# Storing two images interleaved, column by column, so that a depthwise matmul reads 8 rows of 64 instead of 16 rows of 32

## What is computed

```python
# x: (8, 32, 64, 64) f32
xd    = concat of x[:, :, i::2, j::2] for i, j in (0,1)      # (8, 128, 32, 32), of the group-normalised x
feats = concat([dwconv(xd, w1, 1), dwconv(xd, w3, 3), dwconv(xd, w5, 5)], axis=1)   # depthwise, zero padding
y     = einsum('bchw,oc->bohw', feats, w_proj[:, :, 0, 0])   # 384 -> 128 channels
out   = x + (the four 32-channel parts of y put back on the even/odd rows and columns)
```

## Time and profile before

| | us |
|---|---|
| median of 3 runs | 147.49 (147.2 to 148.9) |
| span of the profiled execution | 147.0 |
| PE / DVE / ACT / POOL busy | 133.2 / 117.4 / 103.0 / 98.2 |

### The profile page before, as it was taken

One profiled execution on the slowest core, in us unless ns is written; L12 is line 12 of the kernel. 1 busy time (PEld: TensorE's weight loads), 2 busy tenths in 40 slices (PEclk: granted clock), 3 DMA queues, 4 the chain that ended last, 5 costly groups with the idle time before them and its releaser, 6 DMA issues.

```text
span 147.0 us, 1502 instructions
## 1 busy us (share of the span) xinstructions
PE 133.2 (91%) x513; PEld 98.8 (67%) x513; DVE 117.4 (80%) x132; ACT 103.0 (70%) x110; POOL 98.2 (67%) x73
## 2 busy tenths in 40 slices
PE   0478699999999999999999999999999999999960
PEld 0324487788776777678768777777777778777820
DVE  0198999996299999999999999799929996993051
ACT  2295999999956998699869986998799750005000
POOL 7104799999699529994999399649984998001910
PEclk9999999999999999999999999999999999999997
DMA  3999993052052016001509599025194990936946
GB/s 97 217 207 211 207 210 52 0 112 46 0 116 38 0 38 116 0 4 38 114 2 212 109 196 200 7 51 101 36 214 75 185 195 17 214 76 135 195 99 143
DMA packets 35432, 15.73 MB, mean 107 GB/s; under 512 B 34017, under 2 KB 34145, under 8 KB 35041
## 3 DMA queue, kind: packets, MB, share of 16 engines
q1 hardware_dynamic: 33408, 8.39, 31.6%
q0 software_dynamic: 1440, 7.04, 24.7%
q10 hardware_dynamic: 576, 0.21, 0.6%
HBM read 4.41 MB, written 4.19 MB: 59 GB/s over the span
## 4 chain that ended last, share of the span: by engine, by line
PE 86%; DVE 4%; DMA 3%; ACT 2%; ACTq 1%; issue 1%; DVEq 1%; POOL 0%; POOLq 0%
PE YP L551 76%; PE YP L594 9%; DMA w_sb<-in_L_conv_w_dram 3%; DVE st L424 2%; DVE X L522 1%; ACT G L340 1%; DVE weff L449 1%; DVEq L86 0%; PE SMALL L539 0%; ACT HI L384 0%; PE SMALL L533 0%; POOL rstd L253 0%; ACTq L311 0%; ACTq L312 0%; ACTq L310 0%
## 5 line engine op out<-in xcount | busy, mean ns | idle before, releaser
L275 POOL TENSOR_TENSOR RING_SUM<-RING_SUM,PROD 128x900 f32<-128x900 f32 (+1 forms) x37 | 75.1, 2030 | 7.8 <-ACT PROD L365 3.9
L489 DVE SCALAR_TENSOR_TENSOR ACC<-G,coef,ACC 128x930 f32<-128x930 f32 (+1 forms) x62 | 74.2, 1197 | 2.0
L551 PE MATMUL YP<-LO,whi 128*128 128x512 f32 (+1 forms) x154 | 41.6, 419 | 0.0
L551 PE MATMUL YP<-HI,whi 128*128 128x512 f32 (+1 forms) x154 | 40.1, 411 | 1.4 <-ACT HI L384 1.4
L551 PE MATMUL YP<-HI,wlo 128*128 128x512 f32 (+1 forms) x154 | 38.9, 401 | 0.0
L551 PEld LDWEIGHTS YP<-HI,whi 128*128 128x128 f32 x154 | 30.2, 197 | 10.2 <-DVE whi L468 2.6
L365 ACT ACTIVATE PROD<-G,coef 128x900 f32<-128x900 f32 (+1 forms) x37 | 36.2, 1056 | 0.0
L551 PEld LDWEIGHTS YP<-LO,whi 128*128 128x128 f32 x154 | 29.2, 190 | 10.1 <-issue 3.4
L551 PEld LDWEIGHTS YP<-HI,wlo 128*128 128x128 f32 x154 | 29.1, 190 | 7.2
L375 ACT ACTIVATE Y<-YP 64x1024 f32<-64x1024 f32 x14 | 15.3, 1094 | 23.9 <-PE YP L594 23.8
L340 ACT ACTIVATE G<-X,nbias,rstd 64x1024 f32<-64x1024 f32 (+2 forms) x18 | 21.9, 1214 | 2.1 <-DVE nbias L442 1.7
(11 more groups left out here) (55 smaller groups left out, 57.3 us busy)
## 6 DMA issues: line engine op xcount, KB each, us to landing
LO<-G POOLq DMA_DIRECT2D x7, 543.0 KB, 4.9
X<-in_x_dram SPq DMA_DIRECT2D x12, 256.0 KB, 5.4
X<-Y POOLq DMA_DIRECT2D x3, 1024.0 KB, 7.0
out_dram<-X SPq DMA_DIRECT2D x12, 256.0 KB, 5.9
X<-in_x_dram SPq DMA_DIRECT2D x8, 128.0 KB, 4.3
out_dram<-X SPq DMA_DIRECT2D x8, 128.0 KB, 2.2
wp_sb<-in_L_conv_w_proj_dram ACTq DMA_DIRECT2D x1, 192.0 KB, 3.4
w_sb<-in_L_conv_w_dram ACTq DMA_DIRECT2D x1, 12.5 KB, 3.9
```

The costliest lines, as they stand in the source:

```text
L275: pool.tensor_tensor(dst, dst, prod(b, k), ALU.add).then_inc(prod_added, 1)
L489: dve.scalar_tensor_tensor(part(ACC, tap), g_tap(b, tap), of5(tap), part(ACC, tap), ALU.mult, ALU.add).then_inc(acc_step, 1)
L551: mm = nc.tensor.matmul(dst, w[:, n, :], src, start=start, stop=False, skip_group_check=True)
```

## The change

- `G`, `HI` and `LO` have two slots of a pair each in place of four slots of an image each. The two images of a pair are interleaved: element (row, column, image), so a row is 64 elements (`ROW`) at a pitch of 68, and a tap's column shift is 2 elements per column.
- The unit of work is half of a pair's rows: unit u = 2t is rows 0 to 15 of both images of pair t, unit 2t + 1 rows 16 to 31. A unit has as many columns as an image had, two banks of 8 rows of 64.
- `normalise(t)` handles a pair with four instructions, writing every second element; `split(t)` handles a pair with one instruction for `HI` and one for `LO`; `low_part(t)` has one DMA for a pair. Pair 0 is normalised in three parts, of 9, 8 and 15 rows.
- `copy_y(u)` has four instructions of half the size (64 x 512), reading every second element of PSUM. DVE's and SP's last steps are in twice as many parts of half the size for the lower rows.
- The order on ACT becomes the one shown below: one `normalise`, `split` for two units, and each `copy_y` has a new place.

```diff
-            for b in range(1, B):
-                if b >= 3:
-                    copy_y(b - 3)
-                if b in (2, 4):
-                    act.wait_ge(stats_ready, b // 2 + 1)
-                normalise(b, 0, PH, g_ready)
-                split(b)
-                products(b)
-            copy_y(B - 3)
-            copy_y(B - 2)
+            normalise(0, 0, TOP, g_top)
+            high_part(0, 0, TOP, g_top, 4, hi_top)
+            normalise(0, TOP, MID, g_mid)
+            high_part(0, TOP, MID, g_mid, 4, hi_mid)
+            normalise(0, MID, PH, g_ready)
+            high_part(0, MID, PH, g_ready, 4, hi_ready)
+            products(0)
+            products(1)
+            act.wait_ge(stats_ready, 2)
+            normalise(1, 0, PH, g_ready)
+            split(1)
+            products(2)
+            copy_y(0)
+            products(3)
+            for t in range(2, PAIRS):
+                copy_y(2 * t - 3)
+                if t == 2:
+                    act.wait_ge(stats_ready, 3)
+                normalise(t, 0, PH, g_ready)
+                split(t)
+                products(2 * t)
+                copy_y(2 * t - 2)
+                products(2 * t + 1)
+            copy_y(UNITS - 3)
+            copy_y(UNITS - 2)
...
+            def copy_y(u):
+
+                act.wait_ge(conv_done, u + 1)
+                t, r0 = u // 2, UH * (u % 2)
+                if t >= 2 and u % 2 == 0:
+                    act.wait_ge(row_added[t - 2], 16)
+                yp = YP[:, u % 2, :].rearrange("p (h w b) -> p h w b", w=PW, b=2)
+                for par in range(2):
+                    for j in range(2):
+                        act.activation(Y[HALF * par:HALF * (par + 1), t % 2, r0:r0 + UH, :, j],
+                                       yp[HALF * j:HALF * (j + 1), :, :, par], ACT.Copy).then_inc(y_copied, 1)
...
# add_tap, first tap of units 0 and 1 on DVE
-                    dve.wait_ge(g_ready, 2 * b + 2)
+                    dve.wait_ge(g_ready, 4 * (b // 2) + 4)
...
# tap_matmuls
-                    r0, r1 = span(dy, bank * BANK_ROWS, (bank + 1) * BANK_ROWS)
-                    src = image(tile, b, (r0 + dy) * PITCH + 2 + dx, r1 - r0)[:, :, c0:c1]
-                    dst = YP[:, b % 2, r0 * PW:r1 * PW].rearrange("p (r c) -> p r c", c=PW)[:, :, c0:c1]
+                    r0, r1 = span(dy, base + bank * BANK_ROWS, base + (bank + 1) * BANK_ROWS)
+                    src = pair(tile, t, (r0 + dy) * PITCH + 2 * (2 + dx), r1 - r0)[:, :, c0:c1]
+                    dst = YP[:, b % 2, (r0 - base) * ROW:(r1 - base) * ROW].rearrange("p (r c) -> p r c", c=ROW)[:, :, c0:c1]
...
# high(b)
-                    for bank, rows_ready in enumerate([hi_top, hi_ready]):
+                    for bank, rows_ready in enumerate([hi_top, hi_mid]):
...
-                    pe.wait_ge(hi_ready, b + 1)
+                    pe.wait_ge(hi_ready, b // 2 + 1)
                     if b >= 2:
-                        pe.wait_ge(y_copied, 2 * (b - 1))
+                        pe.wait_ge(y_copied, 4 * (b - 1))
```

More of the change, by code:

```diff
@@ L45 @@
 N_PROD = [len(taps) - 1 for taps in POOL_OF]
[L46 removed]
+PROD_SIZE = UH * ROW
 LATE = (0, 1)
@@ L82, in span, with unit_rows, unit_cols @@
     return max(lo, -d), min(hi, PH - d)
+def unit_rows(u, dy):
+    r0 = UH * (u % 2)
+    lo, hi = span(dy, r0, r0 + UH)
+    return lo - r0, hi - r0
+def unit_cols(dx):
+    c0, c1 = span(dx, 0, PW)
+    return 2 * c0, 2 * c1
 def build(nc, x, w1, w3, w5, wp, out):
@@ L331, in _ @@
             act.activation(whi[:, N_INNER:N_PE, :], weff[:, N_INNER:N_PE, :], ACT.Copy).then_inc(extra_ready, 1)
-            def normalise(b, r0, r1, done):
-                if b >= SLOTS:
-                    act.wait_ge(f_ready, b - SLOTS + 1)
-                    act.wait_ge(lo_ready[b - SLOTS], 16 if b > SLOTS else 1)
-                t, p0 = b // 2, HALF * (b % 2)
-                rows = X[p0:p0 + HALF, t, r0:r1, :].rearrange("p h (w j) -> p h w j", j=2)
-                for j in range(2):
-                    act.activation(g_image(b, r0, r1)[HALF * j:HALF * (j + 1)], rows[:, :, :, j], ACT.Identity,
-                                   bias=nbias[p0:p0 + HALF, t:t + 1],
-                                   scale=rstd[p0:p0 + HALF, t:t + 1]).then_inc(done, 1)
@@ L368, in copy_y, with normalise @@
-            def copy_y(b):
-                act.wait_ge(conv_done, b + 1)
-                if b >= 4:
-                    act.wait_ge(row_added[b // 2 - 2], 16)
-                p0 = HALF * (b % 2)
-                for j in range(2):
-                    act.activation(Y[p0:p0 + HALF, b // 2 % 2, :, :, j],
-                                   YP[HALF * j:HALF * (j + 1), b % 2, :].rearrange("p (h w) -> p h w", w=PW),
-                                   ACT.Copy).then_inc(y_copied, 1)
+            def normalise(t, r0, r1, done):
+                if t >= SLOTS:
+                    act.wait_ge(f_ready, 2 * (t - SLOTS) + 2)
+                    act.wait_ge(lo_ready[t - SLOTS], 16 if t > SLOTS else 2)
+                for par in range(2):
+                    p0 = HALF * par
+                    rows = X[p0:p0 + HALF, t, r0:r1, :].rearrange("p h (w j) -> p h w j", j=2)
+                    for j in range(2):
+                        dst = g_image(t, r0, r1)[HALF * j:HALF * (j + 1)].rearrange("p r (c b) -> p r c b", b=2)
+                        act.activation(dst[:, :, :, par], rows[:, :, :, j], ACT.Identity,
+                                       bias=nbias[p0:p0 + HALF, t:t + 1],
+                                       scale=rstd[p0:p0 + HALF, t:t + 1]).then_inc(done, 1)
@@ new lines, in products @@
+            def products(u):
+                if u - SUMS in LATE:
+                    act.wait_ge(f_ready, u - SUMS + 1)
+                elif u > SUMS:
+                    act.wait_ge(acc_step, steps_before(u - SUMS) + 1)
+                act.activation(RING_SUM[:, u % SUMS, :, :], g_tap(u, POOL_OF[u][0], True), ACT.Copy,
+                               scale=of5(POOL_OF[u][0])).then_inc(first_prod, 1)
+                for k in range(N_PROD[u]):
+                    if products_before(u) + k >= PRODS:
+                        act.wait_ge(prod_added, products_before(u) + k - PRODS + 1)
+                    act.activation(prod(u, k), g_tap(u, POOL_OF[u][k + 1]), ACT.Copy,
+                                   scale=of5(POOL_OF[u][k + 1])).then_inc(prod_ready, 1)
@@ L611, in _ @@
             pe.wait_ge(whi_ready, 1)
-            for b in range(B):
+            for b in range(UNITS):
                 high(b)
```

211 lines of the change are left out of this document (107 added, 104 removed).

## The result

The changed kernel takes 156.96 us (median of 4 runs, 156.54 to 157.77); the kernel before, run beside it on the same chip, takes 148.19. The ratio is 1.060, 95% interval 1.054 to 1.067; ratios compare the means of a kernel's fast runs, without runs more than 1.5% above its fastest, so they can differ a little from the ratio of the medians. The profiled execution has a span of 155.5 us where that of before has 147.0: 8.5 us more. The forecast was 154.0, in a range of 150.5 to 158.5.

What follows compares the result with a forecast made beforehand. PE's matmul spacing was taken to bound the kernel. `high(2)` at 54.4, `high(4)` 85.0, `high(6)` 115.6, `ring(7)` 145.95 and the tail gave a span of 153.5, 6.5 more; on the median 147.49 that is 154.0 us, range 150.5 to 158.5.

Steps and rivals of the forecast that it cites:

- The direction and its mechanism: Whole kernel: slower, 6.5 us more, with PE idle before `high(2)`, `high(4)` and `high(6)` until released by ACT's copy.
- ACT's chain: ACT's queue from `ring(2t - 3)` to `high(2t)`: copies, normalise, split and six products, 20.45 us, and 0.1 to release PE.
- The two unknown forms: Normalise's strided writes and the copy's strided PSUM reads on ACT: nothing added; upper bound for the reads 0.58 us a unit.
- Length of the pauses: PE's waits at `high(4)` and `high(6)` for ACT's copies: about 2.8 us each.
- PE's own part: PE from that ring to `high(2t)`: low 4.06, high 8.13, ring 1.72, low 4.06, in all 17.97 us.
- The start: Up to `high(2)`: pair 0 normalised whole and pair 1's scale late, so `high(2)` starts at 54.4, 4.85 us late.
- The matmuls: PE's tap matmuls: half the row breaks save 13.4 ns each, a unit's taps taking 12.19 us instead of 12.91.
- the rows cost nothing: Rival on PE's tap matmuls: they don't get faster, + 192 x 13.4 ns, 156.6 us; chance 0.10.
- The tail: From `ring(7)` to the end: DVE's eight smaller adds 3.5 us instead of 2.85, stores smaller, +0.55 us.
- The clock: Rival on PE's new pauses: each brings 3 us at 1.2 GHz, three cost 4.2 us, 158.2 us; chance 0.10.
- pairs: From `high(2)` to `high(4)` and on to `high(6)`: 30.6 us a pair, where two images took 29.24.
- last stretch: From `high(6)` to `ring(7)`, PE setting the pace: 31.94 us less 120 matmuls of 13.3 ns, 30.35 us.

Runs made afterwards that it cites:

- the pattern experiment: The changed kernel with the nine inner taps of units 1 to 7 reading different patterns of 512 elements; one unbroken run took 232 ns a matmul, no kernel time given.
- e10_widths: The changed kernel with the inner taps of units 1 to 7 reading one aligned contiguous run, 256 to 512 elements wide; matmuls of 256 columns stood 118 ns apart.

## Why the prediction was right, point by point

**The direction and its mechanism: right.** PE pauses before `high(2)`, `high(4)` and `high(6)`, each released by `copy_y`; taking each place away gives the time back.

**ACT's chain: right.** Worked out 20.45 us and 0.1 for PE, measured 20.26 and 0.14. Strided writes and strided PSUM reads cost nothing to speak of: copies of 512 start every 0.65 us (four in 2.59), where 0.67 was taken. The two unknown forms at the lower bound were the right choice.

**Length of the pauses: a third too long.** 2.8 us foreseen, 1.72 and 1.83 measured. The chain on ACT was right; PE's own part was worked out with matmuls that are too fast. With 12.74 instead of 12.19 us a unit PE's 16.25 us of tap matmuls become 16.98, and ACT's chain was 0.19 shorter: 2.8 - 0.73 - 0.19 = 1.9. So the pauses came out shorter than foreseen through the error in the matmuls, not through one in the queue. The pair took 30.87 and 30.96 us for 30.6.

**The start: right in kind, 1.5 us too long.** `G` was complete and DVE began at 23.17 (23.6 foreseen); PE waited 1.76 us at the combine (2.7); ACT waited for the scale of pair 1:

```profile
36.13 5.45 ACT L370 ACTIVATE G<-X,nbias,rstd 64x1024 f32<-64x1024 f32 x4 [2.38 <-DVE nbias L484]
```

at 36.13 for 37.5 foreseen. From the first tap to the end of the scale DVE took 12.93 us instead of the 13.78 carried over from before, where one short instruction between the taps (`dev`, 128 x 1) had taken 1.40 us; here it took 0.16, against which stood a wait of 0.44 for POOL's rstd. That one term makes 0.85 of the 1.5 us, the first tap 0.4, and ACT's own chain most of the rest.

**The matmuls: wrong, the step that failed.** "I take 13.4, since the contiguous record has no such excess": that was a record of the ring's f32 matmuls, taken for the rounded type of the taps. An unbroken run of the taps' type costs 232 ns by the pattern experiment, not 216, so 16 of the 27 ns put down to the rows were never theirs, and of the rest only part goes, since the shifted taps left the 16-byte boundary. A unit gained 0.17 us, not 0.72. The rival "the rows cost nothing", 156.6 with a chance of 0.10, hit the measured 156.96 in its sum, though not for its reason: rows do cost, by where they start. The Trainium skill (Advanced Engine Details and Errata, SBUF Cachelines) has lines of 16 bytes in SBUF and a penalty when each access goes to a different one; the boundary seen here agrees with that, the 240 to 250 ns at pitch 34 for every start do not follow from it. Its figure of 216 ns for 512 columns (TensorE: Matmul & The Clock Gate, Back-to-back issue gap), which it gives for a single matmul, was not reached by any pattern, 229 being the least mean of a group.

**The tail: right in sign, mis-sized.** +0.55 us was written, +2.15 measured. DVE's eight adds took 3.60 as worked out (3.5). The term was closed with "the stores behind them are smaller". Smaller they are, but there are twice as many, SP takes 0.50 us to issue each of the last ones, and ends 2.8 us after DVE. The number of issues was in the diff, and their rate was never asked for.

**The clock: not in the pauses of the changed kernel.** Its three pauses of 0.64 to 1.83 us before `high(2)`, `high(4)` and `high(6)` and the one of 1.76 us at the combine brought no stretch at half clock. It has one, at the start, behind 2.35 us in which PE waited for `HI` and 1.2 us of matmuls at full clock (window, length, engines, PE clock, DMA share, GB/s):

```profile
18.00:21.40 3.40, 3.40 (x9) 2.21 (x8) 0.00 (x0) 3.31 (x5) 1.67 (x2) 0.50 1.36 209
```

There matmuls of 512 columns stood 427 ns apart, and the first 18 took 6.18 us; before, where six of them stood 400 to 427 ns apart, they took 5.83. PE then had 1.76 us to spare at the combine, so this cost nothing. The pause at the combine was followed by half clock in two of the experiments (1.66 and 1.77 us), one of 2.41 us was, and so were those of 3.87 and 6.84 us with the narrower matmuls (`e10_widths`, 384 columns 320 ns apart); one of 2.36 was not. So the rival was worth its chance of 0.10; which pause brings the clock down can't be told from its length alone, and no run here settles it.

**The errors set against each other.** On the span: start -1.5, pairs +0.6, last stretch +1.2, tail +1.6, in all +2.0 (153.5 foreseen, 155.5 measured). The median lies another 1 us above: the 0.49 us by which the median of before was over its span was no property of the kernel; the executions that were timed and profiled at once took some 1.8 us more than their span (157.29 for 155.5; a run of the kernel before with a span of 147.0 took 148.75). The profile of before was thus of a run above its median of 147.49.

## What to carry to other kernels

A change that makes the unit of work on one engine larger must be followed through the queue that releases its buffers: here the pair as the unit of work put 15 us of strictly ordered work (65.98 to 81.04) between two copies that had had 10.7 between them, and half of the products behind it instead gave both pauses back. Price a matmul from a record of the same type and pattern, and when rows are merged see where each row starts, not only how many there are. Count DMA issues at the end of a kernel: where they follow one another without a gap, bytes divided by the time of one issue is the bandwidth.

## What the runs showed of the hardware

- A row break in the moving operand was nearly free where every row starts on a 16-byte boundary, with 16 rows as with 8 (233 to 238 ns against 232 for one run), and up to 32 ns a matmul for 16 rows elsewhere.
- Matmuls on rounded f32, reading one unbroken run, stood 229 to 236 ns apart at 512 columns and 147 at 320; from 256 to 512 columns that was 11 to 23 ns over their columns at 2.4 GHz.
- SP issued a 64 KB store every 0.50 us where nothing held it, and one queue so moved 130 GB/s; with two queues, and the stores of the pair before still under way, 204 GB/s were moved.
- A DVE step with two SBUF inputs took 3.20 instead of 1.29 us when an add on POOL ran as it came up; once POOL waited for it, it took 1.29 again, without a gain in time.
- Half clock followed PE pauses of 1.66, 1.77, 2.35, 2.41, 3.87 and 6.84 us, and not others of 1.76, 1.83 and 2.36.
